# Split maxima padded to 128 columns and turned by a DMA transpose instead of by TensorE; SyncE's queue and GpSimd's order rearranged around it

## The reference

```
q = rope(layernorm(x) @ Wq); k, v = split(ctx @ Wkv); k = rope(k)        # 32 heads of 16
w = softmax(q k^T / sqrt(16)); x = x + (w v) @ Wout + bout
h = gelu(bitlinear(layernorm(x), w_fc)); x = x + bitlinear(h, w_proj)     # hidden width 2048
bitlinear(x, w): layer_norm of x, clipped at its absolute maximum, times sign(round(w / mean|w|)) * mean|w|
```

## Time and profile before

| | before |
|---|---|
| median of three runs | 802.49 us (801.60 to 803.46) |
| profiled execution | 800.98 us |
| its span | 799.1 us |
| projection and early scores | 0 to about 146 us |
| attention loop with scores, s = 2 to 31 | about 146 to 497 us |
| last steps and feed-forward | about 497 to 799 us |
| TensorE busy | 773.6 us, 97% of the span |
| SyncE's DMA queue | 115.44 MB, 58.9% of 16 engines |

### The profile page before, as it was taken

The page is one execution under the profiler, slowest core; times in us unless marked ns, Lnnn a source line. Parts: engine busy times, 40 slices in busy tenths (PEclk is TensorE's granted clock), DMA queues, the critical chain, the costliest instruction groups (busy, mean ns, idle before and its releaser), DMA issues.

```text
span 799.1 us, 11757 instructions
## 1 busy us (share of the span) xinstructions
PE 773.6 (97%) x3844; PEld 332.4 (42%) x3844; DVE 674.0 (84%) x945; ACT 462.0 (58%) x843; POOL 340.2 (43%) x446
## 2 busy tenths in 40 slices
PE   5899999899999999999999999899999999999998
PEld 3788876223322222222222222244444444444443
DVE  7788998788888888888888888269999999998895
ACT  5677775577777777777777777734322333223430
POOL 4787776764355455445445544323222121111000
PEclk9999999799999999999999999999999999999999
DMA  8488996555456555765666583226456644555446
GB/s 286 143 219 240 260 278 154 118 146 137 111 148 173 149 136 143 146 144 156 172 160 173 158 170 84 80 56 139 106 112 142 129 105 93 110 114 106 94 92 132
DMA packets 173743, 116.19 MB, mean 145 GB/s; under 512 B 114626, under 2 KB 145394, under 8 KB 173682
## 3 DMA queue, kind: packets, MB, share of 16 engines
q1 hardware_dynamic: 173682, 115.44, 58.9%
HBM read 64.50 MB, written 25.43 MB: 113 GB/s over the span
## 4 chain that ended last, share of the span: by engine, by line
PE 87%; DVE 6%; ACT 2%; DMA 2%; issue 2%; POOL 1%; SPq 0%; DVEq 0%; POOLq 0%; ACTq 0%
PE banks L723 16%; PE banks L709 15%; PE banks L668 13%; PE banks L977 11%; PE banks L992 11%; PE banks L282 10%; PE banks L963 7%; PE banks L311 2%; PE banks L679 1%; DVE h_stats L1047 1%; ACT probs_words L779 1%; DVE h_scales L1060 1%; PE banks L267 1%; DMA stack_words<-max_rows 1%; DMA stack_words<-stack_words 1%
## 5 line engine op out<-in xcount | busy, mean ns | idle before, releaser
L779 ACT ACTIVATE probs_words<-banks 128x512 f32<-128x512 f32 x512 | 276.2, 597 | 99.9 <-PE banks L709 98.0
L759 DVE TENSOR_REDUCE maxima<-banks 128x2 f32<-128x1024 f32 x240 | 283.1, 1216 | 49.9 <-PE banks L668 49.9
L709 PE MATMUL banks<-stack_words 98*128 98x512 bf16 x512 | 175.0, 385 | 3.7 <-ACT probs_words L779 1.8
L668 PE MATMUL banks<-stack_words 96*128 96x512 bf16 x480 | 144.2, 381 | 0.0
L723 PE MATMUL banks<-probs_words,late_words 128*32 128x512 f32 x1024 | 136.4, 605 | 0.5
L992 PE MATMUL banks<-ternary_words,stack_words 128*128 128x512 f16 x512 | 113.0, 379 | 0.6 <-DMA stack_words<-stack_words 0.6
L977 PE MATMUL banks<-ternary_words,late_words 128*128 128x512 f16 x512 | 113.1, 379 | 0.0
L1155 ACT ACTIVATE probs_words<-probs_words,h_moments 128x2048 f32<-128x2048 f32 (+1 forms) x17 | 32.2, 1901 | 134.4 <-DVE h_moments L1052 134.4
L709 PEld LDWEIGHTS banks<-stack_words 98*128 98x128 bf16 x512 | 39.6, 97 | 144.3 <-ACT probs_words L779 85.1
L796 POOL TENSOR_SCALAR neg_max<-maxima 128x16 f32<-128x16 f32 x32 | 8.3, 258 | 161.7 <-DVE maxima L759 159.9
L992 PEld LDWEIGHTS banks<-ternary_words,stack_words 128*128 128x128 f16 x512 | 50.0, 98 | 64.9 <-issue 6.3
(11 more groups left out here) (145 smaller groups left out, 980.1 us busy)
## 6 DMA issues: line engine op xcount, KB each, us to landing
o_rows<-late_words SPq DMA_DIRECT2D x32, 256.0 KB, 2.7
k_parts<-ternary_words SPq DMA_DIRECT2D x48, 128.0 KB, 3.1
q_parts<-ternary_words SPq DMA_DIRECT2D x48, 128.0 KB, 2.5
stack_words<-q_parts SPq DMA_DIRECT2D x32, 192.0 KB, 2.9
stack_words<-k_parts SPq DMA_DIRECT2D x96, 64.0 KB, 2.7
stack_words<-k_parts SPq DMA_DIRECT2D x32, 192.0 KB, 2.8
attn_words<-in_x_dram SPq DMA_DIRECT2D x16, 256.0 KB, 4.2
probs_words<-in_L_ffn_w_fc_dram SPq DMA_DIRECT2D x16, 256.0 KB, 3.8
```

Of the source, the lines that this page charges most:

```text
L668: mm = self.nc.tensor.matmul(self.score_slot[j % 2][:, i], self.mem.q_stack[0:STACK, slot, head, c * P:(c + 1) * P], self.mem.k_stack[0:ST ...
L709: self.nc.tensor.matmul(self.mem.banks[:, self.ST_BANK[k]], self.mem.k_stack[0:STACK + 2, slot, head, c * P:(c + 1) * P], self.mem.q_stack ...
L759: dve.tensor_reduce(self.maxima[:, g % 2, 2 * j:2 * j + 2], self.score_slot[j % 2], AX.X, ALU.max).then_inc(self.scores_read, 1)
L779: act.activation(self.probs[:, c, head, :], self.mem.banks[:, self.ST_BANK[k]], ACT.Exp, scale=1 / math.sqrt(HEAD)).then_inc(self.exp_done, 1)
```

## The change

The transpose of the split maxima moves from TensorE to a DMA transpose that SyncE issues. [...] `turn_first_max`, `save_max`, the transposes on TensorE and the bf16 identity go. The ring of banks becomes a plain ring of three over all groups. In SyncE's step the turn comes first, then the stacks, then the rows of the maxima, and only then raw weight, sums and the weight's transpose. SyncE now waits twice for the maxima: for the split, and, ahead of the rows, for the turn to have landed. GpSimd splits before it ternarises. TensorE's second step has two new waits, for `x_low_ready` and `ctx_low_ready`, in the place of that for `max_saved`.

```diff
-    HALFWAY = 8
-    RING = [4 + i % 3 for i in range(15)] + [5, 6]
-    TURN_BANK = RING[HALFWAY]
-    ST_BANK = RING[:HALFWAY] + RING[HALFWAY + 1:]
+    ST_BANKS = 3
...
-        self.max_parts = sb("max_parts", [P, 2, 2 * GH * CHUNKS], BF16)
-        self.max_rows = sb("max_rows", [2 * GH * CHUNKS, 2, P], BF16)
+        self.max_parts = sb("max_parts", [P, 2, P], BF16)
+        self.max_rows = sb("max_rows", [P, 2, P], BF16)
...
+    def turn_max(self, sp, g):
+        sp.wait_ge(self.split_ready, g + 1)
+        sp.wait_ge(self.max_padded, 1)
+        if g >= 2:
+            sp.wait_ge(self.max_loaded[(g - 2) % STACK_SLOTS], ((g - 2) // STACK_SLOTS + 1) * DMA)
+        sp.dma_start_transpose(self.max_rows[:, g % 2], self.max_parts[:, g % 2]).then_inc(self.max_turned[g % 2], DMA)
+
     def load_max(self, sp, g):
-        sp.wait_ge(self.max_saved, g + 1)
+        sp.wait_ge(self.max_turned[g % 2], (g // 2 + 1) * DMA)
         sp.dma_start(self.mem.q_stack[STACK:STACK + 2, g % STACK_SLOTS].rearrange("p h (c q) -> p (h c) q", c=CHUNKS),
-                     self.max_rows[:, g % 2]).then_inc(self.max_loaded[g % STACK_SLOTS], DMA)
+                     self.max_rows[0:2 * GH * CHUNKS, g % 2]).then_inc(self.max_loaded[g % STACK_SLOTS], DMA)
...
-        if k != self.after_turn:
-            need(pe, self.exp_done, g * 16 + self.st_before[k] + 1)
-        elif g < GROUPS - 1:
-            pe.wait_ge(self.max_saved, g + 2)
-        else:
-            pe.wait_ge(self.exp_done, g * 16 + self.before_turn + 1)
-        self.nc.tensor.matmul(self.mem.banks[:, self.ST_BANK[k]],
+        need(pe, self.exp_done, g * 16 + k + 1 - self.ST_BANKS)
+        self.nc.tensor.matmul(self.st_bank[(g * 16 + k) % self.ST_BANKS],
...
-            if c == 1 and s <= GROUPS:
-                self.turn_max(pe, s - 1)
...
-        need(pool, self.max_turned, g - 1)
+        need(pool, self.max_turned[r], g // 2 * DMA)
...
                 if s == TILES + 3:
+                    att.turn_max(sp, 0)
                     att.load_max(sp, 0)
...
             for s in range(GROUPS + 3):
+                if 1 <= s - 2 < GROUPS:
+                    att.turn_max(sp, s - 2)
+                if STACK_SLOTS <= s < GROUPS:
+                    att.load_stacks(sp, s)
+                if 1 <= s - 2 < GROUPS:
+                    att.load_max(sp, s - 2)
                 if 2 <= s < GROUPS:
                     att.load_weight(sp, w_fc, w_proj, s)
-                if STACK_SLOTS <= s < GROUPS:
-                    att.load_stacks(sp, s)
                 att.pack_sums(sp, s)
-                if 1 <= s - 2 < GROUPS:
-                    att.load_max(sp, s - 2)
...
-                    if k == att.HALFWAY - 1 and within(s - 1, GROUPS):
-                        att.save_max(act, s - 1)
...
+            pool.memset(att.max_parts[:, :, 2 * GH * CHUNKS:P], 0.0).then_inc(att.max_padded, 1)
...
+                if 2 <= s < GROUPS:
+                    att.split_maxima(pool, s)
                 if s < GROUPS:
                     att.ternarise(pool, s)
-                if 2 <= s < GROUPS:
-                    att.split_maxima(pool, s)
```

More of the change, by code:

```diff
@@ L538, in __init__ @@
         self.neg_max = sb("neg_max", [P, 2, GH * CHUNKS], F32)
-        self.max_parts = sb("max_parts", [P, 2, 2 * GH * CHUNKS], BF16)
-        self.max_rows = sb("max_rows", [2 * GH * CHUNKS, 2, P], BF16)
+        self.max_parts = sb("max_parts", [P, 2, P], BF16)
+        self.max_rows = sb("max_rows", [P, 2, P], BF16)
         self.score_slot = [banks[:, 0:2], banks[:, 2:4]]
         self.early_bank = banks[:, 7]
-        self.early_max_bank = banks[0:2 * GH * CHUNKS, 1, CTX:CTX + P // 2].bitcast(BF16)
         self.pv_bank = banks[:, 7]
-        st = self.ST_BANK
-        self.st_before = [max(j for j in range(k - 16, k) if st[j % 16] == st[k]) for k in range(16)]
-        self.before_turn = max(k for k in range(self.HALFWAY) if st[k] == self.TURN_BANK)
-        self.after_turn = min(k for k in range(self.HALFWAY, 16) if st[k] == self.TURN_BANK)
-        self.max_bank = banks[0:2 * GH * CHUNKS, self.TURN_BANK, 0:P // 2].bitcast(BF16)
+        self.st_bank = [banks[:, 4 + i] for i in range(self.ST_BANKS)]
         self.stacks_loaded = [sem(f"stacks_loaded_{i}") for i in range(STACK_SLOTS)]
         self.max_loaded = [sem(f"max_loaded_{i}") for i in range(STACK_SLOTS)]
+        self.max_turned = [sem(f"max_turned_{i}") for i in range(2)]
         self.inverse_loaded = [sem(f"inverse_loaded_{i}") for i in range(2)]
@@ L660, in scores @@
         if g == self.EARLY and j == 0:
-            pe.wait_ge(self.max_saved, 1)
+            pe.wait_ge(self.prj.x_low_ready, TILES)
+            pe.wait_ge(self.prj.ctx_low_ready, TILES)
         if g == self.EARLY and j == 1:
@@ L778, in exponentials @@
             need(act, self.pv_done, (g - 1) * CHUNKS + c + 1)
-        act.activation(self.probs[:, c, head, :], self.mem.banks[:, self.ST_BANK[k]], ACT.Exp,
+        act.activation(self.probs[:, c, head, :], self.st_bank[(g * 16 + k) % self.ST_BANKS], ACT.Exp,
                        scale=1 / math.sqrt(HEAD)).then_inc(self.exp_done, 1)
-    def save_max(self, act, g):
-        act.wait_ge(self.max_turned, g + 1)
-        if g >= 2:
-            act.wait_ge(self.max_loaded[(g - 2) % STACK_SLOTS], ((g - 2) // STACK_SLOTS + 1) * DMA)
-        act.copy(self.max_rows[:, g % 2], self.max_bank if g else self.early_max_bank).then_inc(self.max_saved, 1)
     def split_maxima(self, pool, g):
@@ L1471, in _ @@
         def _(pool):
-            for n, square in enumerate((mem.ident, mem.identb)):
-                pool.memset(square[:], 0.0).then_inc(filled, 1)
-                pool.wait_ge(filled, 2 * n + 1)
-                pool.affine_select(out=square[:], in_=square[:], compare_op=ALU.not_equal, fill=1.0, base=0,
-                                   pattern=[[-1, P]], channel_multiplier=1).then_inc(filled, 1)
+            pool.memset(mem.ident[:], 0.0).then_inc(filled, 1)
+            pool.wait_ge(filled, 1)
+            pool.affine_select(out=mem.ident[:], in_=mem.ident[:], compare_op=ALU.not_equal, fill=1.0, base=0,
+                               pattern=[[-1, P]], channel_multiplier=1).then_inc(filled, 1)
             pool.memset(prj.row_ones.bitcast(mybir.dt.uint32), 0x3F803F80).then_inc(prj.row_ones_set, 1)
             pool.memset(mem.half_power[:], -0.5).then_inc(prj.power_set, 1)
+            pool.memset(att.max_parts[:, :, 2 * GH * CHUNKS:P], 0.0).then_inc(att.max_padded, 1)
             pool.wait_ge(prj.power_set, 1)
```

19 lines of the change are left out of this document (2 added, 17 removed).

## The result

| | before | changed |
|---|---|---|
| median (lowest to highest) | 802.11 us (799.89 to 803.46), 6 runs | 795.70 us (794.21 to 797.79), 6 runs |
| the profiled execution | 800.98 us, span 799.1 | 797.79 us, span 795.9 |

The ratio is 0.9921 [0.9903, 0.994]: 6.4 us faster, where 9.4 were forecast. The profiled execution of the changed kernel is the slowest of its six. In it TensorE is granted 0.66 of full speed from 25 to 30 us, and the first weighing of v starts at 152.78 us, where a later profile of the same kernel, granted 1.00 there, has it at 151.34. Two later series gave the changed kernel 0.9949 [0.9921, 0.9978] and 0.9932 [0.9915, 0.9948].

The account below looks back on a forecast made before the run. TensorE's queue was taken to bound the attention loop. The terms 7.8 + 0.3 + 0.7 + 0.5 + 0.5 - 0.4 = 9.4 us, taken off the median of 802.5, gave 793.1 us, with a range of 790.5 to 799.0.

Parts of the forecast that it names:

- the third rival: Attention loop: six to ten of 29 steps late by 0.5 us, 3 to 5 us lost; 797 us, chance 0.13.
- TensorE's queue bounds, 30 x 0.26 us: Attention loop, steps 2 to 31: removing TensorE's transpose of the maxima shortens each step by 0.26 us, 7.8 us in all.
- In the loop that costs nothing: Attention loop: matmuls k = 8, 9, 14 and 15 waiting for the exponential two back cost 0 us there.
- 0.7 us in s = 32 and 33: Steps 32 and 33: with a plain ring of three, a matmul goes out before its wait, saving 0.35 us in each.
- The first group's transpose, 0.3 us: Before the loop: the first group's transpose and its wait for GpSimd's split leave TensorE's chain, saving 0.3 us.
- 0.5 us at step 3: Step 3: rows of the maxima come sooner, so TensorE's 1.25 us stall shrinks by 0.5 us; bounds 0 and 1.25.
- 0.5 us for the late load of the earlier trace: Loop, rows issued at 317.75: no quotient between split and rows any more, 0.5 us back; bounds 0 and 0.7.
- -0.4 us for late loads: Attention loop: a load or two come late on the thinner margin, 0.4 us lost; bounds 0 and 9.
- The turn's price: SyncE's queue: the 128-column DMA transpose of the maxima takes 1.2 us to issue and 2.4 us to land.
- The second rival: Attention loop: rows or stacks come too late in every step, slower than before, up to 813 us; chance 0.09.
- The fourth: SyncE's queue: waiting on the turn delays the weights' turns until the expansion waits for them; 802 us or more, chance 0.02.
- The rule against the change: Transposes: the skill's 390 ns on TensorE against 1309 ns by DMA would mean an estimated 28 us lost.

Follow-up runs that it names:

- the small matmul alone: Changed kernel plus one unused 32-column matmul on TensorE in the transpose's old place, three-deep ring kept: 802.18 us, ratio 1.0006.
- the ring's waits alone: Changed kernel with matmuls k = 8, 9, 14 and 15 again waiting for the exponential two back: 800.96 us, ratio 0.9992.
- the quotients apart: Changed kernel with the numerators loaded one step ahead of the inverses, 256 KB in each step: 792.82 us, repeated 793.17 us.

## Why the prediction came out as it did

The time, 795.7, lies inside the range, 2.6 us over the forecast of 793.1. What came is not the forecast's own case but the third rival (the margin fails now and then, 797), which had a chance of 0.13; the range held because it had been drawn to take that rival in. By stretches, from the profiles of before and of the changed kernel's third series, both granted 1.00 from 25 to 30 us:

| us | before | changed | gone | forecast |
|---|---|---|---|---|
| up to the first weighing of v | 151.09 | 151.34 | -0.25 | 0.3 |
| four blocks, step 3 in them | 13.04 | 12.96 | 0.1 | 0.8 |
| the other 114 blocks of the loop | 331.67 | 328.08 | 3.6 | 7.6 |
| all behind them | 303.34 | 302.11 | 1.2 | 0.7 |

- **TensorE's queue bounds, 30 x 0.26 us.** Right in size: the blocks that are not late are 2.84 us, and 8.4 us of longer blocks (7.7 by the transpose's block, the rest the late load of the earlier trace rows) are gone. The rival with 0.16 per step falls with the 3.10 of the small matmul alone. Incomplete in its cause, see the next point.
- **"In the loop that costs nothing", of the ring.** This step failed, and nothing in the total shows it. In the kernel before it is true (3.10 us with the ring's waits and without them), but the waits cost 0.20 us per step once the transpose is gone. The 7.8 us came out right only because the change removed both, which is luck.
- **0.7 us in s = 32 and 33.** Right: 0.32 or 0.33 in each. The run with the ring's waits alone brought exactly these back. The other 0.6 us behind the loop were not forecast: in the profile of before TensorE waits once near its end for a DMA of the feed-forward, 0.56 us, and in those of the changed kernel it does not. Why is open; the wait is 0.21 us with the order alone and 0.81 with the small matmul alone.

```profile
785.29 10.53 PE L992 MATMUL banks<-ternary_words,stack_words 128*128 128x512 f16 x48 [0.56 <-DMA stack_words<-stack_words]
```

- **The first group's transpose, 0.3 us.** Not found. The first weighing of v begins at 151.09 us before, and at 151.2 to 153.6 in the twelve profiles of kernels with the change's head. It moves from execution to execution, so 0.3 us can be neither shown nor refuted, but a gain is nowhere to be seen.
- **0.5 us at step 3.** This step failed: the new order frees the rows, and the DMA turn takes it back. The forecast had the turn land 2.4 us after its issue, so that the rows went out 0.3 us sooner. In the eleven profiles with both the DMA turn and the new order it landed in 3.4 to 4.2 us, and TensorE stood 0.9 to 1.4 us for the rows in eight of them, 0.2 in one. In the other two, the changed kernel's first profile among them, nothing stands there, but the block two ahead is 4.5 to 4.6 us long instead of 2.84: TensorE was still at its half level, 1.2 GHz (granted 0.56 and 0.67 from 151 to 157 us, where the profile of before has 1.00), and that gave the rows the time. With the order alone, where the turn is TensorE's, the four blocks are 1.4 us shorter. SyncE's queue and TensorE in the third profile of the changed kernel:

```profile
154.78 1.16 SPq L592 DMA_TRANSPOSE max_rows<-max_parts  x1
158.40 0.72 SPq L596 DMA_DIRECT2D stack_words<-max_rows  x1
...
160.49 0.39 PE L692 MATMUL banks<-stack_words 98*128 98x512 bf16 x1 [1.44 <-DMA stack_words<-max_rows]
```

- **0.5 us for the late load of the earlier trace rows.** Right: no quotient stands between split and rows any more, and this place is not late. But that was the wrong place to look, see the next point.
- **-0.4 us for late loads.** This term was mis-sized: 4.8, 3.3 and 4.8 us in three profiles. The step of it that failed is the landing of the rows, "behind them at some +10". In the steps that were late they were issued 4.6 to 6.0 us behind the turn, where 4.3 were forecast, and took 4.2 to 4.9 us to land, not 3.0. The trace of before held the warning, and not in the earlier trace rows alone: by the semaphores, from 170 to 490 us the rows landed in 1.9 to 2.1 us in the steps without quotients ahead and in 3.0 to 5.7 in all twelve with them. I took the 5.69 for an effect of what stands directly ahead in the queue. The quotients in the changed kernel are a whole step back, with 3 us and a weight's transpose between, and still reach the turn and the rows behind it. Put in with 4.3, the mean of the three profiles, for 0.4, the sum is 5.5 us and the forecast 797.0; without the 0.3 and 0.5 us above that were not found it is 4.7 and 797.8. The three series measured 6.4, 4.2 and 5.5 us. The versions with quotients spread or cut gave 792.3 to 793.2.
- **The turn's price.** Issue 1.12 us against 1.2 taken, shortest landing 2.2 against 2.4. Both are right as the price in a quiet queue. But 2.4 was put in for every step, and behind quotients the turn mostly took 2.8 to 6.0 in the three profiles.
- **The second rival** (late in every step) did not come: its line, rows that land 4.4 us after issue, was crossed only in steps behind quotients. **The fourth**, SyncE falling behind through its wait on the turn, did not occur in the changed kernel, where that wait is 0.6 us in the step shown above. The run with the stacks first, 832.7 us, has that wait at full length, at landings of the turn up to 7.2 us with nothing to hide them.
- **The rule against the change**, TensorE's turn as the shorter one. Shorter it is, 0.23 us against at least 2.2. In a queue with no gap it was worth its 0.26 us for each, and the DMA's longer way is free as long as the margin of 3.8 us for the rows holds. Four to seven steps of 29 did not hold it. The rule and this kernel differ in what they count, and the runs side with the queue.

What stays open: that it is the eight engines through which the quotients hold up the rest. A version of both loads with an outermost dimension of 128, the rows of the inverses still read 16 times, would tell.

## What to carry to other kernels

When TensorE's queue is full, a small operation in it costs its block's lengthening, and a wait that lies in the same block can cost nearly as much and be hidden by it: take both out, and price each by putting it back alone. A chain of two DMAs that replaces an on-chip step should be priced with the landings seen in the fullest stretch, each of its links, and with every large transfer issued in the last 9 us ahead of it (the distance from the quotients to the rows here), not only with those that stand directly before it in the queue. If such a transfer comes in every second step, half of it in every step may fit where the whole does not.

## What the runs showed of the hardware

- A large load reaches past transfers that were issued behind it. With two loads of 256 KB issued at 296.92 and 297.58, the next transpose, issued at 298.21, took 7.6 us to land, the one at 301.03 took 5.2, and the rows at 306.23 4.8. The Trainium skill, page "DMA: Bandwidth & Descriptors", section "Queues, rings and completion order", has all of SyncE's transfers on one ring of each DMA engine, and the descriptors on each engine consumed in ring order. The trace agrees in that the three landed in the order of their issue, at 305.8, 306.2 and 311.0.
- The same number of bytes can cost the engines very different time: packets of 176.6% of 16 engines' time in 3.6 us against 81.5%, by the shape of one load of 256 KB.
- The outermost dimension of a load shows in its semaphore: 9 updates for the loads with an outermost dimension of 8, 3 for the rows, which go to two partitions, 16 for the turns, stacks and weights. Two loads of 256 KB with 9 updates landed in 4.4 to 4.9 us by their medians, whether each row was read once or 16 times; two with 16 updates in 3.0 to 3.2.
- Turns of about 4 us also occur in steps without quotients. In several of these, packets of the instruction queues (16 KB one) fall into the turn's flight. In the first profile with the quotients apart, the turn issued at 298.96 has none in its 2.3 us and lands in 2.2, that at 310.31 has two and lands in 4.0 (the DMA table of these 2.3 us):

```profile
q1 hardware_dynamic: 349, 0.08, 16.4%
q8 instruction: 1, 0.02, 3.2%
q14 instruction: 1, 0.01, 0.9%
```

There are turns of 2.3 us with such a packet too, so this is a coincidence seen often and not a cause shown.
- The issue of one load of a stack (64 to 192 KB) takes 0.42 us on SyncE as a rule and at the longest 1.90 before the change and 1.86 after it.
